# Softmax stage of a two-layer attention and experts kernel: the turned scores of a slot issued ahead of its relative product and scores

## The reference, cut to what matters

```
att_rel_pos = jnp.einsum('bhsd,pd->bhsp', q, pos_emb_k)
att_idxs = jnp.clip(ar[None, :] - ar[:, None], -r, r - 1) % P      # r = 128
att_pos = att_rel_pos[:, :, ar[:, None], att_idxs]
attn_val = jnp.einsum('bhqd,bhkd->bhqk', q, k)
att = jax.nn.softmax((attn_val + att_pos) * attn_scale, axis=-1)
y = jnp.einsum('bhqk,bhkd->bhqd', att, v)
```

## Time and profile before

| | |
|---|---|
| median of 3 runs | 1165.86 us (1160.58 to 1168.11) |
| the profiled execution, its time | 1161.36 us |
| its span | 1159.6 us |
| softmax stage, lead-in and steady part | 428 to 451 us, 451 to 916 us of the span |
| granted TensorE clock, mean over the span | 0.96 |
| busy: PE, DVE, ACT, POOL | 89%, 65%, 63%, 46% |

### The profile page before, as it was taken

The page is one execution under the profiler, slowest core; times in us unless marked ns, Lnnn a source line. Parts: engine busy times, 40 slices in busy tenths (PEclk is TensorE's granted clock), DMA queues, the critical chain, the costliest instruction groups (busy, mean ns, idle before and its releaser), DMA issues. The chain is left out here.

```text
span 1159.6 us, 22263 instructions
## 1 busy us (share of the span) xinstructions
PE 1035.2 (89%) x7828; PEld 652.0 (56%) x7828; DVE 753.9 (65%) x1682; ACT 728.6 (63%) x1087; POOL 535.7 (46%) x692
## 2 busy tenths in 40 slices
PE   1499999999898957999999999999999889999997
PEld 1344444677676644555555545455454466878785
DVE  6245242478475637777888888877777157676776
ACT  1289988556353524777777777777775655555553
POOL 1166676576353410444444553343222187655564
PEclk9999999999898955999999999999999999999999
DMA  5621141643536656888888898888763376433333
GB/s 129 236 88 51 59 126 32 150 121 115 149 109 182 211 209 215 236 243 230 236 237 257 256 267 231 251 236 239 249 212 100 93 221 141 121 117 120 117 125 90
DMA packets 143345, 197.40 MB, mean 170 GB/s; under 512 B 31744, under 2 KB 109553, under 8 KB 143201
## 3 DMA queue, kind: packets, MB, share of 16 engines
q1 hardware_dynamic: 124898, 185.50, 51.4%
q0 software_dynamic: 18336, 10.48, 5.6%
HBM read 123.00 MB, written 72.74 MB: 169 GB/s over the span
## 5 line engine op out<-in xcount | busy, mean ns | idle before, releaser
L1022 DVE TENSOR_REDUCE a_part<-a_duo 128x2 f32<-128x1024 f32 (+3 forms) x256 | 215.5, 855 | 13.5 <-PE a_duo L895 11.9
L692 POOL DMA_DIRECT2D scr_y1c<-ys x240 | 123.9, 524 | 209.8 <-DVE ys L1003 206.3
L1015 DVE CUSTOM_DVE_ANT_0 a_band_sum<-a_duo,a_rel_raw 128x256 f32<-128x256 f32 (+2 forms) x320 | 131.4, 448 | 77.1 <-PE a_duo L895 57.2
L1442 POOL TENSOR_TENSOR f_hid_lo<-f_hid,att 128x512 fp32r<-128x512 f32 (+1 forms) x100 | 129.6, 1297 | 104.5 <-ACT att L1413 104.2
L655 ACT ACTIVATE a_probs<-a_duo 128x1024 f32<-128x1024 f32 x192 | 139.8, 828 | 21.6 <-PE a_duo L604 20.1
L895 PE MATMUL a_duo<-att 31*128 31x512 f32 (+3 forms) x672 | 145.0, 427 | 8.7 <-DVE a_part L1022 4.0
L908 PE MATMUL a_duo<-att 32*128 32x512 f32 (+3 forms) x672 | 137.9, 408 | 14.9 <-DVE a_part L1022 12.7
L1571 DVE TENSOR_TENSOR f_hid<-f_u,w_share 128x512 f32<-128x512 f32 (+1 forms) x168 | 116.2, 692 | 50.3 <-DMA w_share<-scr_cw 29.2
L975 ACT ACTIVATE a_rel<-a_rel_ps 128x384 f32<-128x384 f32 x240 | 117.5, 490 | 46.6 <-PE a_rel_ps L882 45.9
L1442 POOL TENSOR_TENSOR f_hid_lo<-f_hid,f_hid_hi 128x512 fp32r<-128x512 f32 x68 | 88.1, 1296 | 89.1 <-ACT f_hid_hi L1413 89.0
L593 POOL TENSOR_TENSOR a_probs<-a_probs,const 128x256 f32<-128x256 f32 x128 | 99.9, 798 | 58.3 <-ACT a_probs L655 58.1
(11 more groups left out here) (272 smaller groups left out, 2056.8 us busy)
## 6 DMA issues: line engine op xcount, KB each, us to landing
a_rel_raw<-scr_rel SPq DMA_DIRECT2D x128, 384.0 KB, 4.5
scr_rel<-a_rel SPq DMA_DIRECT2D x120, 384.0 KB, 3.6
w_share<-scr_cw SPq DMA_DIRECT2D x144, 128.0 KB, 3.2
w_share<-scr_cw SPq DMA_DIRECT2D x44, 256.0 KB, 3.2
att<-scr_q SPq DMA_DIRECT2D x40, 96.0 KB
scr_y1c<-ys POOLq DMA_DIRECT2D x240, 8.0 KB, 3.6
w_share<-scr_cw SPq DMA_DIRECT2D x20, 192.0 KB, 2.8
w_share<-scr_cw SPq DMA_DIRECT2D x16, 224.0 KB, 3.1
```

Source lines behind the costliest of these rows:

```text
L692: eng.dma_start(scr["y1c"][w, b, head, :, at:at + T // 4], sb["ys"][32 * (2 * hd + c) + HD * w:32 * (2 * hd + c) + HD * (w + 1), h % 2, :] ...
L1015: ins = dve.tensor_tensor_reduce(band_sum[:, m % 2, hd, 0:wide], both[:, hd, (a - 4 * x) * P:(b - 4 * x) * P], rel_raw[:, e % RING, hd, (a ...
L1022: ins = dve.tensor_reduce(part[:, h % 2, x, :, j % 4], both[:, :, lo * P:hi * P], AX.X, ALU.max, negate=True)
L1442: pool.tensor_tensor(hid_lo[0:m, n % 4, :], hid[0:m, n % 2, :], f32(hid_hi[0:m, n % 4, :]), ALU.subtract).then_inc(lo_ready, 1)
```

## The change

In TensorE's program T moves ahead of O and S of the same slot; B and V stay where they are. The numbering of the jobs follows: T(n), S(m), T(n+1), S(m+1). So T(n) now takes the bank pair of S(m - 2) and waits for VectorE's reduction of it, and S(m) takes that of T(n - 1) and waits for ScalarE's exponential of slot n - 1. Nothing is added or removed, no instruction changes its shape, and the other engines' programs stay as they are.

```diff
@@ job_of @@
         for n in slots:
+            if 0 <= n < SLOTS:
+                job_of["t", n] = len(job_of)
             if 0 <= n + LS < SLOTS:
                 job_of["s", n + LS] = len(job_of)
-            if 0 <= n < SLOTS:
-                job_of["t", n] = len(job_of)
@@ block.tensor @@
-                if AHEAD <= r < SLOTS:
-                    offsets(r)
-                if 0 <= m < SLOTS:
-                    scores(m)
                 if 0 <= n < SLOTS:
                     if n % 8 == 0:
                         pe.wait_ge(row_stored[n // 8 % 2], 32 * (n // 16 + 1))
                     free_pair("t", n)
                     t_last = turned(n)
+                if AHEAD <= r < SLOTS:
+                    offsets(r)
+                if 0 <= m < SLOTS:
+                    scores(m)
                 if 0 <= n < SLOTS:
                     (turned_band(n) or t_last).then_inc(st_ready, 1)
```

## The result

The changed kernel takes **1289.9 us** (median of four runs, 1275.7 to 1301.7) against 1167.0 us before: ratio 1.101, 95% interval 1.089 to 1.113. In some executions of any of these kernels the granted clock is lower and the time some per cent longer; the ratios here leave such executions out, the medians and ranges of times don't. The forecast was 1219 us with a range to 1238. The direction was right, and the loss is about twice as large: 114 us between the profiled executions, against 58.

A forecast was written before the change was run, and what follows sets the result against it. TensorE bounds the steady part, held back by waits for VectorE. Per period 25.40 own work + 6.36 stalls + 1.41 row chain = 33.17 us against 29.29; 15 x 3.88 = 58 us on 1161.4 gives 1219 us, range 1193 to 1238.

The forecast's parts named there:

- ScalarE's ring: B ends, exponential, S, next B, next exponential: 2.20 us around, stalls summing to 6.36 us a period; chance 0.78.
- The stalls: TensorE's waits at S: 0.96 us behind a slot with B and no V, 0.39 behind B and one V.
- the handover: From the exponential's end on ScalarE to S on TensorE: taken as 0.05 us, 0.15 as the dearer case.
- the row chain: VectorE copies turned rows after the late S's reduction; TensorE waits 0.52 us at slot 4, 0.89 at 12, together 1.41.
- rival 3: TensorE's rests in nine of 16 slots bring the clock down: 55 us on top, 1274 us; chance 0.04.
- The limit between 59% and 94% busy: TensorE's busy share at which the clock falls; the rows did not show where, with 83% forecast after the change.
- the clock's rival: The same as rival 3: the clock falls, 55 us on top, 1274 us; chance 0.04.
- A quarter of the 240 slots: Share of slots rival 3 put at the lower clock, at 0.9 us more a slot: 55 us on top.
- The first (relief wins): At S of the nine stalling slots the wait is mostly hidden: faster, 1118 us were the stalls nil; chance 0.04.
- the fourth (it does not bite): VectorE and ScalarE trade places one for one, or bank pairs come free in another order: within 1%, 1161 us; chance 0.05.
- The second (small stalls vanish): V and the next front overlap more, row chain stays: 30.9 us a period, 1186 us; chance 0.09.
- The rule on row groups: Matmuls in different row groups run at once, so the order of S and T would be free and cost nothing.

The follow-up runs named there:

- Experiment 3: Changed kernel with an exponential of 512 columns in place of 1024, leaving out each pair's second head: 1171.9 us profiled, ratio 1.010 to the kernel before.
- Experiment 7: Changed kernel with VectorE's row copy ahead of the maxima and T computed twice in all nine slots where S waits: 1217.4 us, ratio 1.043 to the kernel before.
- Experiment 8: Changed kernel with VectorE's row copy ahead of the maxima and B ahead of S in TensorE's slot: 1195.0 to 1290.8 us, no ratio.
- experiment 5: Changed kernel with VectorE's copy of the turned rows ahead of the maxima of the same slot: 1233.5 us, ratio 1.057 to the kernel before.
- experiment 9: Kernel before the change with another spread of the V products over the 16 slots: 1196.7 us profiled, ratio 1.028 to the kernel before.
- experiment 1: Changed kernel's order of issue (T, O, S) with the old numbering of the bank pairs: 1294.6 and 1315.5 us.
- experiment 6: Changed kernel with VectorE's row copy ahead of the maxima and T computed twice in slots 0, 3, 5, 7, 14: 1226.7 to 1241.3 us, ratio 1.063.
- experiments 1 and 2: The second is the kernel before with only the new numbering of the bank pairs, issue still O, S, T: 1279.8 and 1296.2 us, ratio 1.104.

## Why the prediction was right and wrong

**Right, and a little more than half of the loss: ScalarE's ring.** The stalls came where they were forecast and at their price (1.0 and 0.4 us against 0.96 and 0.39), the handover was 0.05 us as taken, the row chain grew (waits of 20.1 us against 1.41 x 15 = 21), T's matmuls wait for VectorE's reduction no more, and the period where the clock is up is 33.43 us against 33.17. Experiment 3 shows the exponential's length in the ring. Experiment 7 gives the time of the ring with the clock held up, on the shorter row chain: 1217 us. Experiment 8, in the periods where its clock was up, agrees in part with B standing behind S as the ring's other half.

**Wrong: the clock, which the sum has at nothing.** The forecast is for "The clock at 1.00 in the stage"; it was 0.86, and that cost 49.7 us in 14 periods. The step that failed is "Against it: no rest will be over 1 us" in rival 3. I had rows in which TensorE is busy 59% and the clock at its lower level, forecast 83%, and wrote that where the limit lies these rows do not show; then I gave the rival 0.04 on the length of single rests. That argument fails twice. There are rests over 1 us (1.25, from the 14th pair on), and the spells didn't need them: 13 of 15 begin behind rests of 0.68 to 0.88 us and smaller ones alone. With the row waits shortened 5 spells were left (experiment 5), and with the rests of S filled as well, down to 0.45 us and less, there was none (experiment 7).

The rests are a cause, then, but neither the length of one nor the busy share over a long stretch told here when the clock falls. Spells began behind a single rest of 1.40 us, but also behind three of at most 0.32 (experiment 9), while rests of 1.27 us passed without one (experiment 3). TensorE was busy 93% of 360 us in experiment 9, with eight spells in them, 92% of 480 us in experiment 7 with none, 91% of 420 us in experiment 3 with none, and 73% of 35.5 us in experiment 1 with the clock at 1.00. The limit between 59% and 94% busy that the prediction looked for is not seen. The Trainium skill's sentence ("TensorE: Matmul & The Clock Gate", Part 1: The HAM clock gate), that activity releases the throttle, agrees with experiment 7, which added matmuls whose results are computed twice and gained 16 us over the same kernel without them; experiment 6, with five of the nine, gained nothing. Experiment 8 doesn't bear it out: busy 201 of 204 us, and the clock stayed at 0.50.

**The range** left out the case that came. It ended at 1238 because the clock's rival was given less than it needed to be let in; the forecast and that rival together would have given 1219 + 55 = 1274, and the profiled execution took 1275.7. That this is so close is partly luck: the price of a slot at the lower level was worked out from rows, but its "A quarter of the 240 slots" had no row behind it.

**The rivals.** The first (relief wins) and the fourth (it does not bite) are out by the result, and experiments 1 and 2 add that neither half of the change is harmless. The second (small stalls vanish) is out by slot 2's 0.40 us. The rule on row groups that the prediction quotes from the Trainium skill ("TensorE: Matmul & The Clock Gate", Part 3: Packing small matmuls) holds for matmuls that may start: at slot 4 T and S start 0.02 us apart (530.46 and 530.48). In slot 3 S has to wait and starts 1.18 us after T.

**What stays open.** Which stretch brings the clock down, in exact terms, and how much of it is chance. In experiment 6 spells began only in the late pairs, four of five in slot 3, where the filled rest leaves one of 0.45 us; filling four small rests elsewhere took these spells away too. Why experiment 8 stayed at the lower level for so long. And how much of the changed kernel's spread (1275.7 to 1301.7 us) is in the number of spells: only one of its runs has a trace.

## What to carry to other kernels

Before moving an instruction ahead of another in a queue, write down the ring that the wait behind it closes: the readout's length, plus all that stands between its end and the next readout. A readout that overlaps the next slot cost nothing here. Of one that stands in a ring, each pass costs what the engine's other work doesn't cover (here 1.0 or 0.4 us), and whatever is taken off its length comes back in every stalling slot (experiment 3). Changing the order of issue without the order of the buffers, or the reverse, only chose here whose readout it is.

Rests of TensorE have a second price. In a stage with short matmuls, sum what the rests cost at the upper clock, and then take the same stage with a share of it at the lower one as a forecast of its own, with a real chance, as soon as the change adds rests to every period. In this kernel rests of 0.45 to 0.88 us were enough, and no length was found below which the clock is safe.

When a spread by hand is tuned against one wait (here V over the slots), every other engine that waits for the same product has to be in the sum: the spread that ignored one was 2.8% slower, the one that kept it 1.3% faster.

## What the runs showed of the hardware that was not expected

The granted clock fell behind a single rest of 1.40 us in a stage 93% busy, behind groups of rests with none over 0.88 us (the changed kernel), and three times at slot 4 of experiment 9, with no rest over 0.32 us ahead, two of these for 17 us. It doesn't fall each time: in experiment 9 the rest of 1.40 us recurs in every pair at the same slot, and the clock fell there in eight of 14 pairs; in experiment 3 it fell behind none of four rests of 1.27 us.

After the lead-in of experiment 8, TensorE was busy 201 of 204 us and the clock stayed at 0.50, up to 680 us of the span. The kernels with S ahead of B left the lower level 8 to 34 us into the steady part. A period of experiment 8's kernel takes 50.8 us at the lower level and 31.2 at the upper, a ratio of 1.63 and not of two: at the lower level TensorE waits for only 3 of 204 us.
